# Experts one tile further behind the gates, and all transposes of a period in one run

## The reference, cut to what matters

```python
gh = h @ W_hh.T + b_hh                      # h: normalised x, 512 -> 3 x 512
h_r, h_z, h_n = jnp.split(gh, 3, axis=1)
r = jax.nn.sigmoid(i_r + h_r)               # i_*: what the edges brought
z = jax.nn.sigmoid(i_z + h_z)
n = jnp.tanh(i_n + r * h_n)
h_new = (1.0 - z) * n + z * h
x1 = x + h + (gamma * (h_new - run_mean) * jax.lax.rsqrt(run_var + BN_EPS) + beta)
h2 = _layernorm(x1)
gate_logits = h2 @ Wg + bg                  # 8 experts, the best two weighted by a softmax
hid = comb * relu(h2 @ W1 + b1)             # 8 experts x 32 columns, and a shared one of 32
out = x1 + hid @ W2 + b2 + 0.5 * shared
```

## Time and profile before

| | us |
|---|---|
| median of 3 runs | 1514.01 (1510.68 to 1516.63) |
| the profiled execution | 1514.16 |
| its span, first to last instruction | 1512.4 |
| TensorE busy (matmuls) | 1405.1 (93%) |
| VectorE busy | 1107.0 (73%) |
| GpSimd busy | 926.7 (61%) |
| ScalarE busy | 608.9 (40%) |

### The profile page before, as it was taken

One profiled execution on the slowest core, in us unless ns is written; L12 is line 12 of the kernel. 1 busy time (PEld: TensorE's weight loads), 2 busy tenths in 40 slices (PEclk: granted clock), 3 DMA queues, 4 the chain that ended last, 5 costly groups with the idle time before them and its releaser, 6 DMA issues. The chain is left out here.

```text
span 1512.4 us, 23117 instructions
## 1 busy us (share of the span) xinstructions
PE 1405.1 (93%) x6780; PEld 1142.3 (76%) x6780; DVE 1107.0 (73%) x2777; ACT 608.9 (40%) x1100; POOL 926.7 (61%) x1049
## 2 busy tenths in 40 slices
PE   3689799999749999999999999999999999999995
PEld 2578588887637888888888887888888888888884
DVE  2863334323438888888888888888888888888885
ACT  2341213112114544444445444444454444444541
POOL 3111340200338778788887887877878878778771
PEclk9899899999879999999999999999999999999997
DMA  6422242325522233322223333222333232222320
GB/s 192 126 68 95 66 134 88 111 98 164 156 108 82 101 102 102 101 93 92 92 97 101 100 101 102 92 91 94 99 101 98 98 101 95 95 95 97 101 89 28
DMA packets 76097, 152.92 MB, mean 101 GB/s; under 512 B 34802, under 2 KB 36704, under 8 KB 75939
## 3 DMA queue, kind: packets, MB, share of 16 engines
q0 software_dynamic: 45056, 79.02, 16.4%
q1 hardware_dynamic: 31008, 73.48, 14.8%
HBM read 115.67 MB, written 36.66 MB: 101 GB/s over the span
## 5 line engine op out<-in xcount | busy, mean ns | idle before, releaser
L1412 PE MATMUL bank<-whh_hi,h_hi 128*125 128x512 f32 x960 | 391.6, 408 | 20.5 <-DVE h_lo L472 20.5
L1412 PE MATMUL bank<-whh_hi,h_lo 128*125 128x512 f32 x960 | 380.2, 396 | 0.0
L1412 PE MATMUL bank<-whh_lo,h_hi 128*125 128x512 f32 x960 | 379.7, 396 | 0.0
L1412 PEld LDWEIGHTS bank<-whh_hi,h_hi 128*125 128x125 f32 x960 | 178.9, 186 | 58.5 <-DVE h_lo L472 20.9
L1412 PEld LDWEIGHTS bank<-whh_hi,h_lo 128*125 128x125 f32 x960 | 178.4, 186 | 44.0
L1412 PEld LDWEIGHTS bank<-whh_lo,h_hi 128*125 128x125 f32 x960 | 179.4, 187 | 38.4
L1158 POOL DMA_INDIRECT gates<-gates_in,slot_at x80 | 129.1, 1614 | 78.2 <-POOL slot_at L1156 65.3
L1250 ACT ACTIVATE hn_raw<-bank 125x512 f32<-125x512 f32 x80 | 47.9, 598 | 280.4 <-PE bank L1412 280.4
L1197 POOL TENSOR_TENSOR h_n<-h,n_gate 125x512 f32<-125x512 f32 x80 | 104.3, 1304 | 59.5 <-ACT n_gate L1278 59.5
L1183 POOL TENSOR_TENSOR hn<-hn_raw,hn_bias 125x512 f32<-125x512 f32 x80 | 103.5, 1294 | 30.7 <-ACT hn_raw L1250 30.5
L1092 PE MATMUL bank<-wih_hi,a_hi 128*125 128x512 f32 x240 | 98.5, 411 | 24.5 <-DVE g_out L855 10.5
(11 more groups left out here) (176 smaller groups left out, 3214.9 us busy)
## 6 DMA issues: line engine op xcount, KB each, us to landing
xt<-in_x SPq DMA_DIRECT2D x80, 250.0 KB
out<-y SPq DMA_DIRECT2D x80, 250.0 KB
gates_in<-g_out SPq DMA_DIRECT2D x18, 750.0 KB
wih_lo_raw<-in_wih_t SPq DMA_DIRECT2D x4, 768.0 KB, 23.1
whh_lo_raw<-in_whh_t SPq DMA_DIRECT2D x4, 768.0 KB, 17.4
gates_in<-late_out SPq DMA_DIRECT2D x2, 750.0 KB
gates<-gates_in,slot_at POOLq DMA_INDIRECT x80, 10.8
m_lo_raw<-in_attr_t SPq DMA_DIRECT2D x5, 250.0 KB, 6.9
```

Source lines behind the costliest of these rows:

```text
L1412: last = pe.matmul(to[0:R, :], a[:, s, k * R:(k + 1) * R], w[:, k, q * D:(q + 1) * D], start=n == 0, stop=n == 3 * DK - 1)
```

## The change

Three things are changed. The experts' tiles are counted one further back: h2's transposes, its high and low part, f1 and the choice of experts work on tile t - 2 instead of t - 1, and hid, f2, y and the store on t - 3 instead of t - 2. On TensorE the transposes of h2, hid and h now stand in this order in one run between the products of n and those of z. ScalarE copies the high parts in the same order. One more period is added at the end, and eight instead of four tiles are written out ahead of the loop. VectorE's order is the same, with other tiles.

The diff, cut to what the steps speak of:

```diff
-    FIRST, UNROLL = 4, 4
+    FIRST, UNROLL = 8, 4
...
-        for j in range(NT + 2 - FIRST - UNROLL * LOOPS):
+        for j in range(NT + 3 - FIRST - UNROLL * LOOPS):
...
 # ScalarE: the copies of h2 and hid now ahead of that of h
+                if p.has(-2):
+                    act.wait_ge(h2_turned, t - 1)
+                    wait_from(act, f1_prod, t - 2)
+                    act.activation(h2_hi[:, :], b_th2[:, 0:DK * R], ACT.Copy).then_inc(h2_hi_done, 1)
+                if p.has(-3):
+                    act.wait_ge(hid_turned, t - 2)
+                    wait_from(act, f2_prod, t - 3)
+                    act.activation(hid_hi[:, :], b_thid[:, 0:KF * R], ACT.Copy).then_inc(hid_hi_done, 1)
...
 # TensorE
+                if p.has(-2):
+                    pe.wait_ge(h2_done, t - 1)
+                    wait_from(pe, h2_lo_done, t - 2)
+                    turn(pe, b_th2, h2[:, p.slot(-2), :], DK).then_inc(h2_turned, 1)
+                if p.has(-3):
+                    pe.wait_ge(hid_done, t - 2)
+                    wait_from(pe, hid_lo_done, t - 3)
+                    turn(pe, b_thid, hid[:, p.slot(-3), :], KF).then_inc(hid_turned, 1)
                 if p.has(1) and not p.first(1):
                     turn_h(pe, p)
                 if p.has(0):
                     wait_from(pe, z_pre_done, t)
-                    gate(p.slot(0), b_z, 1, 0, 2)
-                if p.has(-1):
-                    pe.wait_ge(h2_done, t)
-                    wait_from(pe, h2_lo_done, t - 1)
-                    turn(pe, b_th2, h2[:, p.slot(-1), :], DK).then_inc(h2_turned, 1)
-                if p.has(0):
-                    gate(p.slot(0), b_z, 1, 2, DK).then_inc(z_prod, 1)
-                if p.has(-2):
-                    pe.wait_ge(hid_done, t - 1)
-                    wait_from(pe, hid_lo_done, t - 2)
-                    turn(pe, b_thid, hid[:, p.slot(-2), :], KF).then_inc(hid_turned, 1)
+                    gate(p.slot(0), b_z, 1).then_inc(z_prod, 1)
...
```

More of the change, by code:

```diff
@@ L1142, in body @@
                         .then_inc(x_in[s], 16)
-                if p.has(-3):
-                    store(t - 3, p.slot(-3))
+                if p.has(-4):
+                    store(t - 4, p.slot(-4))
             periods(sp, body)
@@ L1281, in body @@
                     act.activation(z_gate[:, :], z_pre[:, :], ACT.Sigmoid).then_inc(z_done, 1)
-                if p.has(-1):
-                    act.wait_ge(gap_done, t)
-                    wait_from(act, comb2_done, t - 1)
+                if p.has(-2):
+                    act.wait_ge(gap_done, t - 1)
+                    wait_from(act, comb2_done, t - 2)
                     act.activation(weight[:, 0:1], gap[:, :], ACT.Sigmoid).then_inc(weight_done, 1)
@@ L1293, in body @@
                 t = p.t
-                if p.first(-2):
+                if p.first(-3):
                     dve.wait_ge(hid_set, 3)
[L1296 to L1300, removed]
+                if p.has(-3):
+                    s = p.slot(-3)
+                    dve.wait_ge(weight_done, 2 * (t - 2))
+                    dve.wait_ge(comb1_done, 2 * t - 5)
                     dve.tensor_scalar(comb1[:, :], iota8[:, :], top_f[:, 0:1], weight[:, 0:1], ALU.is_equal, ALU.mult)\
@@ L1325, in body @@
                     first_norm(dve, p)
-                if p.has(-1):
-                    dve.wait_ge(h2_hi_done, t)
+                if p.has(-2):
+                    dve.wait_ge(h2_hi_done, t - 1)
                     dve.tensor_tensor(h2_lo[:, :], b_th2[:, 0:DK * R], h2_hi[:, :].bitcast(F32), ALU.subtract)\
                         .then_inc(h2_lo_done, 1)
-                if p.has(-2):
-                    dve.wait_ge(hid_hi_done, t - 1)
+                if p.has(-3):
+                    dve.wait_ge(hid_hi_done, t - 2)
                     dve.tensor_tensor(hid_lo[:, :], b_thid[:, 0:(KF - 1) * R],
@@ L1395, in body @@
                     dve.tensor_tensor(r_pre[:, :], b_r[0:R, :], gates[:, s, 0:D], ALU.add).then_inc(r_pre_done, 1)
[L1396 to L1400, removed]
+                if p.has(-3):
+                    s = p.slot(-3)
+                    dve.wait_ge(f2_prod, t - 2)
+                    wait_from(dve, y_stored[s], 16 * p.turn(-3))
+                    dve.tensor_tensor(y[:, s, :], b_f2[0:R, :], x1[:, p.slot4(-3), :], ALU.add).then_inc(y_done, 1)
             periods(dve, body)
@@ L1429, in body @@
                     wait_from(pe, z_pre_done, t)
-                    gate(p.slot(0), b_z, 1, 0, 2)
-                if p.has(-1):
-                    pe.wait_ge(h2_done, t)
-                    wait_from(pe, h2_lo_done, t - 1)
-                    turn(pe, b_th2, h2[:, p.slot(-1), :], DK).then_inc(h2_turned, 1)
-                if p.has(0):
-                    gate(p.slot(0), b_z, 1, 2, DK).then_inc(z_prod, 1)
-                if p.has(-2):
-                    pe.wait_ge(hid_done, t - 1)
-                    wait_from(pe, hid_lo_done, t - 2)
-                    turn(pe, b_thid, hid[:, p.slot(-2), :], KF).then_inc(hid_turned, 1)
[L1441 to L1445, removed]
+                    gate(p.slot(0), b_z, 1).then_inc(z_prod, 1)
+                if p.first(-2):
+                    pe.wait_ge(f_lo_done, 3)
+                if p.has(-2):
+                    pe.wait_ge(h2_lo_done, t - 1)
+                    wait_from(pe, f1_done, t - 2)
                     n = 0
@@ L1452, in body @@
                     last.then_inc(f1_prod, 1)
-                if p.has(-2):
-                    pe.wait_ge(hid_lo_done, t - 1)
-                    wait_from(pe, y_done, t - 2)
+                if p.has(-3):
+                    pe.wait_ge(hid_lo_done, t - 2)
+                    wait_from(pe, y_done, t - 3)
                     n = 0
```

32 lines of the change are left out of this document (13 added, 19 removed).

## The result

The changed kernel takes 1622.48 us (median of 4 runs, 1617.31 to 1623.43), the one before 1513.23 in the same series: a ratio of 1.071 with a 95% interval of 1.068 to 1.075. It is 109 us slower; 117 were forecast, and 1622 lies in the range. The profiled execution took 1617.31 us, its span is 1615.5.

The account below looks back on a forecast made before the run. TensorE, 99.35 of 100 us busy in the loop, was taken to bound, VectorE nearly as full. 76 x 1.47 = 112, plus 7 (drain), minus 2 (start), gave 117 over 1514: 1631 us; own range 1618 to 1648, with rivals 1540 to 1665.

Parts of the forecast that it names:

- The mechanism: TensorE reaches hid's transposes 7.39 us after the first layer, hid comes at 9.28; the wait closes a 14.62 us loop.
- The loop's term: Period 14.62 us instead of 13.15, 1.47 more in each of 76 periods from tile 4 on: 112 us.
- the last step of hid is 1.29 us long in every period: VectorE's 41-column last hid step waits for GpSimd's hn: 1.29 us kept, against 0.20 at its least.
- the first rival: VectorE's last hid step starts ahead of GpSimd's hn: chain 8.19 us, period 13.53, time 1548 us; chance 0.14.
- The ends: Added drain round +7 us (bounds 0 and 9.7), later first layer at the start -2, longer unrolled part 0.
- The 0.33 us wait for h2's low half: TensorE's wait ahead of the experts' first layer goes, since h2's transposes lie more than a z product ahead.
- TensorE's own period: Products, transposes and both layers on TensorE alone, without waits, sum to 12.7 us a period, 0.45 less than before.
- the 0.16 us that one run of transposes should save a period: Merging TensorE's three transpose runs into one drops two exits at 0.08 us each.
- Faster: Rival: hid is there when TensorE reaches it, needing a chain under 7.39 us; period 12.7, time 1485 us; chance 0.07.
- The second collision: Rival: x1 steps against GpSimd push hid's middle step into hn; 1740 us in all periods, 1658 in one of four; 0.10.
- The clock's rival: TensorE standing 1.9 of 14.6 us a period might lower its granted clock; up to 1742 us; chance 0.03.
- The row held against it: A TensorE wait of 2.27 us at 53.44, in the edges' part, left the granted clock at 0.99.

Follow-up runs that it names:

- The shift alone: Changed kernel with TensorE's and ScalarE's order of before, leaving the experts' moved tiles, longer unrolled part and added period; 1519.45 us, 1.004 of the kernel before.
- the one with hid earlier: Changed kernel with VectorE making hid ahead of r's sum and y instead of behind them; 1580.20 us, 1.044 of the kernel before.
- the run alone: Kernel before with all eleven transposes (h2, hid, h) in one run between n and z, experts' tiles as before; 1644.53 us, ratio 1.086.
- the wide step last: Changed kernel with hid's 256-column VectorE step behind its two narrow ones instead of ahead; 1605.14 us, 1.059 of the kernel before.

## Why the prediction was right, and where its sizes were off

*The mechanism* held term by term: the period read above gives 14.70 us for 14.62, its terms each within 0.07. That hid's place is the cause was shown by a step that stands alone: with only hid's transposes and their copy moved back, the loss goes. The shift alone costs nothing, and where the chain was made shorter by leaving hn out, the periods fell by as much.

*The loop's term was mis-sized*: 112 was forecast for 76 periods, 99 measured for 75. From the first to the last of r's sums the loop took 1036.1 us before and 1139.0 after; without the first four intervals (49.0 and 52.8) that is 987.0 and 1086.1 for 75 of them. The step that failed is that the last step of hid is 1.29 us long in every period. One body of four makes it 0.20, at 13.58 us where the first rival said 13.53: about 75 / 4 x 1.04 = 19.5 us less. The three others are 14.75 in the mean, 0.13 over the forecast, which gives back 7.3, and two clock drops 3.1: 75 x 1.47 = 110.3 becomes about 101.

I had given that rival 0.14 as a case for the whole loop. The median of 1.25 in the earlier trace rows spoke for the long step in every period, and rightly for the kernel before: its short steps are those of tiles 1, 75 and 77 to 79 alone. But the change moves VectorE against GpSimd, and a margin of 0.06 us can then come out otherwise in one body and not in another: it should have been taken as a share of the periods, not as all or nothing.

*The ends*: the drain from the last sum of r took 38.1 us, before 35.3: +2.7 for +7, inside the bounds. The first four intervals took 3.8 us more, not 2 less: two of the clock's drops fall there, and in the last of the four, at 16.66 us, the closed loop is at work already. Up to the first sum of r it was 2.5 us less; in the other kernels' traces this sum stands anywhere from 438.8 to 442.9 us, so that is not the change. Together 99.1 + 3.8 + 2.7 - 2.5 = 103.1, the difference of the two spans. The medians lie 109 us apart: the traced run of the changed kernel is the fastest of its four, at a mean granted clock of 0.974, the others' being 0.968 to 0.972, and no trace shows where they spend the rest.

*Two steps were wrong without harm.* The 0.33 us wait for h2's low half does go in the changed kernel, but not because h2's transposes lie further ahead: with them there and hid behind z it stays (12.4 / 38), and with the shift alone too. What follows from the rows is that TensorE's wait for hid takes its place. Hid stands ahead of h2_lo in VectorE's queue, so once TensorE has stood for hid, h2_lo is made while it still has z to do: in the period read it ends at 974.15 + 0.67 = 974.82, and the first layer starts at 976.59.

The other is TensorE's own period, 12.7 us with two exits fewer. Where hid is early on VectorE in the changed kernel, TensorE takes 12.84 us in the short periods from the start of one first layer to the next, with no gap:

```profile
799.91 0.30 PE L1447 MATMUL bank<-f_hi,h_hi 128*125 128x296 f32 x1
...
812.75 0.30 PE L1447 MATMUL bank<-f_hi,h_hi 128*125 128x296 f32 x1
```

In the order of before without hn it took 12.88. So the 0.16 us that one run of transposes should save a period does not show; 0.04 is left of it.

*The other rivals.* Faster: with hn left out the chain was 8.13 us (8.19 in the prediction), 8.33 at the loop's branch, and most periods 13.57 to 13.60; even then TensorE waited 0.64 us (23.6 / 37). The second collision did not come in the changed kernel; it came in the one with hid earlier, with another step. The clock's rival came in small: some 1.6 us in each of the two periods at 610 and 1132 us, the two other drops lying in the first four intervals. The row held against it was too short a view: in the same trace the granted clock is 0.50 from 35 to 45 us and 0.57 from 69 to 77.

*The lock.* The Trainium skill, "SBUF — State Buffer", section "Who interferes with whom", has it that whoever issues first blocks the other whole. The traces agree: 0.20 us or 1.30 for the same step, and hn 0.3 us longer where VectorE's wide step (0.42) won, 0.08 where the narrow one (0.20) did. Who issued first can't be read from starts so close, though: hn is 0.02 us ahead in the period where the narrow step lost, and also 0.02 ahead where the wide step won.

## What to carry to other kernels

Before a step is moved forward on the busiest engine, count the time from where that engine starts the chain to where it will stand for its end, and compare it with the chain's length on the other engine: here 7.4 against 9.3 us, and what was missing came back in each period. Where a short step is long only beside another engine's step, ask which of the two starts first in each body of an unrolled loop, and price it by share. Moving steps to avoid such a meeting can find the next one (it did in all seven kernels here that tried); taking the step out showed what it costs.

## What the runs showed that was not expected

A VectorE step over 8 columns with one tensor input besides its scalars (0.28 us) takes 1.32 beside GpSimd's x_h_b, and a copy over 82 columns (0.20) 1.29. The wide step loses as much (1.52 for 0.42): 1.0 to 1.1 us whatever the width, which weighs most on the smallest steps. The outcome repeated by the body of the unrolled loop, not at random; what sets the 0.02 us between the bodies stays open.

Short drops of the granted clock to 0.50, some 3 us each, came mostly where TensorE waits in every period: 4 in the changed kernel's loop, 10 in the run alone, 16 with the wide step last, 7 with hid early in it, 1 with the shift alone, none in the kernel before from 448 to 1489 us. The changed kernel waits about as long in a period as the run alone (1.44 us, and 48.6 us in 34 periods) and has fewer. Each count is one run's: the traced run of the changed kernel is its fastest, those of the run alone and of the wide step last are their slowest (1652.23 and 1618.72 us), and the other runs' mean clocks are alike (0.968 to 0.972, and 0.968 to 0.970 in the run alone). So whether the kernels differ in this stays open, as does what brings a drop in one period and not in the next.
